# A gated cross-attention block: the scaled rows go through a DMA into a float32r tile and are transposed as float32r

## What is computed

```python
q = einsum('bsd,od->bso', layernorm(x), W) + b
attn_logits = einsum('bqd,bkd->bqk', q, ctx) + (1 - mask) * -1e9
x = x + tanh(g_xattn) * einsum('bqk,bkd->bqd', softmax(attn_logits), ctx)
x = x + tanh(g_ffn) * einsum('bsi,oi->bso', layernorm(x), sign(weight))
```

## Time and profile before

| | |
|---|---|
| three timed runs | 298.51, 302.39, 302.82 us; median 302.39 |
| profiled execution | span 297.0 us; its own time is not listed apart from the three; the median is 5.4 us above the span |
| instructions | 9618 |
| busy shares of the span | PE 96%, PEld 93%, DVE 89%, ACT 87%, POOL 72% |
| granted TensorE clock | mean 0.993 of full speed |
| DMA | 44.40 MB, 149 GB/s over the span |

### The profile page before, as it was taken

The page is one execution under the profiler, slowest core; times in us unless marked ns, Lnnn a source line. Parts: engine busy times, 40 slices in busy tenths (PEclk is TensorE's granted clock), DMA queues, the critical chain, the costliest instruction groups (busy, mean ns, idle before and its releaser), DMA issues.

```text
span 297.0 us, 9618 instructions
## 1 busy us (share of the span) xinstructions
PE 286.3 (96%) x2329; PEld 276.6 (93%) x2329; DVE 265.2 (89%) x1167; ACT 258.8 (87%) x740; POOL 214.6 (72%) x585
## 2 busy tenths in 40 slices
PE   6799999999999999999999999999999999999982
PEld 6789999999999999999999999999999999999972
DVE  4669999999999999999999999999999999999883
ACT  2689999999999999999999999999999999999841
POOL 2546877877787778777777877777787777778543
PEclk9889999999999999999999999999999999999999
DMA  5941464646356544544565453545545444541212
GB/s 130 298 134 42 144 186 152 184 135 186 127 146 184 184 150 146 169 139 146 168 184 154 144 174 125 162 159 184 167 137 174 153 141 146 185 152 70 74 54 89
DMA packets 33539, 44.40 MB, mean 149 GB/s; under 512 B 3504, under 2 KB 17136, under 8 KB 33520
## 3 DMA queue, kind: packets, MB, share of 16 engines
q1 hardware_dynamic: 33520, 44.19, 47.7%
HBM read 27.40 MB, written 16.78 MB: 149 GB/s over the span
## 4 chain that ended last, share of the span: by engine, by line
PE 91%; DMA 2%; SPq 1%; POOL 1%; issue 1%; DVE 1%; ACT 1%; POOLq 0%; ACTq 0%
PE ffn_ps L670 20%; PE pv_ps L652 18%; PE l_ps L636 16%; PE ctx_ps L571 11%; PE xt_ps L604 9%; PE x1t_ps L642 9%; PE pt_ps L617 5%; PE ctx_ps L563 3%; DMA ctx_v<-in_ctx_dram 2%; POOL y L318 0%; POOL rstd L282 0%; DVE x_lo L535 0%; SPq L212 0%; DVE c L524 0%; ACT ffn_scaled L398 0%
## 5 line engine op out<-in xcount | busy, mean ns | idle before, releaser
L282 POOL TENSOR_TENSOR rstd<-ve,minus_half 128x2 f32<-128x2 f32 x128 | 89.1, 696 | 10.0
L636 PE MATMUL l_ps<-m_sb,x_t 128*128 128x77 f32 x512 | 79.0, 258 | 0.3 <-ACT x_t L379 0.3
L344 ACT ACTIVATE xs<-x_in,shift,rstd 128x256 f32<-128x256 f32 x128 | 75.6, 592 | 0.0
L636 PEld LDWEIGHTS l_ps<-m_sb,x_t 128*128 128x128 f32 x512 | 74.8, 191 | 0.6 <-ACT x_t L379 0.6
L642 PE MATMUL x1t_ps<-ident,x 128*128 128x128 f32 x256 | 68.8, 273 | 0.0
L652 PE MATMUL pv_ps<-ctx_v,p_t 77*128 77x256 f32 x256 | 66.1, 380 | 0.0
L670 PE MATMUL ffn_ps<-wf_t,x_hi 128*128 128x256 f32 x256 | 56.2, 301 | 2.5 <-DVE x_lo L535 2.4
L543 DVE SCALAR_TENSOR_TENSOR x<-pv_ps,c,x_in 128x256 f32<-128x256 f32 x128 | 55.5, 475 | 0.4 <-PE pv_ps L652 0.4
L535 DVE TENSOR_TENSOR x_lo<-x1t_ps,x_hi 128x512 fp32r<-128x512 f32 x64 | 44.2, 691 | 12.3 <-ACT x_hi L405 8.8
L318 POOL TENSOR_TENSOR y<-ffn_scaled,x 128x256 f32<-128x256 f32 x64 | 46.6, 728 | 8.2 <-ACT ffn_scaled L398 8.2
L431 DVE BATCH_NORM_STATS2 st<-x_in 128x6 f32<-128x256 f32 x128 | 47.5, 413 | 4.7 <-DMA x_in<-in_x_dram 4.6
(11 more groups left out here) (49 smaller groups left out, 478.9 us busy)
## 6 DMA issues: line engine op xcount, KB each, us to landing
x_in<-in_x_dram SPq DMA_DIRECT2D x64, 256.0 KB, 2.7
out_dram<-y SPq DMA_DIRECT2D x64, 256.0 KB, 2.0
ctx_v<-in_ctx_dram SPq DMA_DIRECT2D x32, 154.0 KB
mask_in<-in_mask_BxSxS_ik_dram SPq DMA_DIRECT2D x32, 154.0 KB, 3.1
wq_raw<-in_L_xattn_W_dram SPq DMA_DIRECT2D x1, 256.0 KB, 2.9
wf_raw<-in_L_ffn_weight_dram SPq DMA_DIRECT2D x1, 256.0 KB, 6.2
bq_col<-in_L_xattn_b_dram SPq DMA_DIRECT2D x1, 1.0 KB, 2.7
g_raw<-in_g_xattn_dram SPq DMA_DIRECT2D x1, 0.5 KB, 3.7
```

What stands on the lines that cost most here:

```text
L282: pool.tensor_tensor(res[:, i], ve[:, i], minus_half[:], ALU.pow).then_inc(res_done, 1)
L344: act.activation(xs[:, n % 2, j], x_in[:, n % N, j], ACT.Identity, scale=rstd1[:, n % R, j:j + 1], bias=shift1[:, n % R, j:j + 1]).then_in ...
L636: ins = pe.matmul(l_ps[:, j * K:(j + 1) * K], x_t[:, r % 2, c, j * P:(j + 1) * P], m_sb[:, c, r % R], start=(c == 0), stop=(c == C - 1))
```

## The change

A second tile `xs_r` of type float32r stands beside `xs`, and a second identity `ident_r` of type float32r. ScalarE still writes `xs`. SyncE then copies the 256 KB of a batch from `xs` to `xs_r` with one DMA, and TensorE waits for that DMA's semaphore and transposes `xs_r` with `ident_r`, with the PSUM tile read as float32r. In slot r the copy of batch r+1 comes first in SyncE's program, ahead of the slot's loads and store; it waits for both activations of `scale_rows` of that batch. VectorE copies the identity once, before its first statistics.

```diff
+        ident_r = sb("ident_r", [P, P], F32R)
+        xs_r = sb("xs_r", [P, 2, T, D], F32R)
+        xs_moved = [sem(f"xs_moved{i}") for i in range(2)]
...
             load_x(0, 4)
 
+            def move_xs(t0, n):
+
+                i = n % 2
+                sp.wait_ge(xs_done, T * (t0 + n + 1))
+                sp.dma_start(xs_r[:, i].bitcast(F32), xs[:, i]).then_inc(xs_moved[i], DMA)
+
+            move_xs(0, 0)
+
             def slot(t0, r):
                 t = t0 + r
+                if exists(t0, r + 1):
+                    move_xs(t0, r + 1)
                 if exists(t0, r + AHEAD):
...
+            dve.wait_ge(ident_ready, 2)
+            dve.tensor_copy(ident_r[:], ident[:]).then_inc(ident_r_ready, 1)
             stats1(0)
...
             def transpose_x(t0, n):
 
-                pe.wait_ge(xs_done, T * (t0 + n + 1))
+                pe.wait_ge(xs_moved[n % 2], landed(t0, n, 2))
                 at_least(pe, xt_done, t0 + n)
                 for c in range(C):
                     for j in range(T):
-                        ins = pe.transpose(xt_ps[:, c, j * P:(j + 1) * P],
-                                           xs[:, n % 2, j, c * P:(c + 1) * P], ident[:])
+                        ins = pe.transpose(xt_ps[:, c, j * P:(j + 1) * P].bitcast(F32R),
+                                           xs_r[:, n % 2, j, c * P:(c + 1) * P], ident_r[:])
                 ins.then_inc(xt_psum, 1)
 
+            pe.wait_ge(ident_r_ready, 1)
             transpose_x(0, 0)
```

More of the change, by code:

```diff
@@ L125, in flamingo_block @@
         half_ready = sem("half_ready")
+        ident_r_ready = sem("ident_r_ready")
         gate_ready = sem("gate_ready")
```

## The result

The changed kernel is slower: 309.29 us median (307.61 to 310.61), the kernel before beside it 301.05 us, a ratio of 1.029 with a 95% interval from 1.021 to 1.037. The forecast was 300.0 us, slightly faster than before; the time is inside the range of 295 to 318, but on the other side. The profiled execution took 310.22 us with a span of 308.2, 11.2 us more than before. That is more than the 8.2 us between the medians. Executions of one kernel differ: nineteen of the kernel before, beside e1 to e4, took 297.7 to 304.5 us, with a mean granted clock of 0.996 in the shortest and 0.972 in the longest. The profile before (clock 0.993) is one of the short ones, the profile after has a mean clock of 0.968.

A forecast was written before the change was run, and what follows sets the result against it. TensorE, busy for 96% of the span, was taken to set the pace. The span of 297.0 less 7.1 (steady slots) plus 4.7 (start) gave 294.6, and 5.4 from span to median made 300.0 us; 80% range 295 to 318.

The forecast's parts named there:

- Part 1: TensorE's four transposes of scaled rows: float32r cuts their spacing from 0.109 to 0.075 us, saving 0.14 us per slot.
- Part 3: Next late engine: TensorE waits about 0.05 us for x1's low part in one slot per pair; 31 pairs save 7.1 us.
- Part 2: Steady slots: SyncE's reaction, a 2.0 us DMA and TensorE's reaction total 2.2 us, fitting the 2.30 us before the transposes.
- the first one: Rival: the copy's DMA lands late, at 2.7 us pairs take 9.20 and the time is 325; chance 0.30 for above 308.4.
- Part 4: Start: the first copy queues behind fourteen start-up DMAs, first transposes at about 13.6 us; costs 4.7 us, between 3 and 6.5.
- 5.4 us from span to median: Amount by which the median before lay above the profiled span, added to the predicted span of 294.6 to give 300.0 us.
- the third rival: TensorE's float32r transposes are slower than plain ones, 0.22 us a piece, adding 26 us, 333 with the start; chance 0.04.

The follow-up runs named there:

- e1: Changed kernel without the copy: ScalarE writes the float32r tile itself, float32r transposes stay; 298.12 us, ratio 0.992 to the kernel before.
- e4: As e3, with ScalarE scaling the rows half a slot sooner and the copy issued ahead of the store; 298.84 us, ratio 0.999 to the kernel before.
- e7: Changed kernel with 50 unread identity transposes filling TensorE's gap ahead of the first batch's transposes; 305.78 us, ratio 1.017 to the kernel before.
- e6: As e4, with the first 24 slots written out instead of the first 8; 298.61 us, ratio 0.992 to the kernel before.
- e5: As e3, with the first 24 slots written out instead of the first 8; 304.48 us, ratio 1.013 to the kernel before.
- e3: Changed kernel, but the first two batches are transposed from xs in float32 without a copy; 303.47 us, ratio 1.012 to the kernel before.
- e8: As e1, with 18 unread identity transposes in TensorE's gap ahead of slot 0; 293.94 us, ratio 0.979 to the kernel before.
- e2: Changed kernel with the copy alone: xs_r is float32 and transposed with the float32 identity; 312.92 us, ratio 1.044 to the kernel before.

## Why the prediction was wrong

**Part 1, the transposes: right in kind, mis-sized.** Where TensorE has waited, the four loads lie in 0.40 us and one lasts 0.142, so they start 0.086 apart instead of the 0.075 taken, within the bounds of 0.067 and 0.12. In an undisturbed slot the first of the three distances stays what it was, 0.130, and the distances behind it fall from 0.108 to 0.086, three of them up to the first feed-forward load. That is 0.07 us a slot where the text had four times 0.034, or 0.14. Part 3's next late engine, the low part of x1, did not show in the steady stretch: the gain there is 0.07 x 62 = 4.3 us instead of 7.1, and the difference is the size of this term. The Trainium skill puts a weight load at its columns / 1.2 ns ("TensorE: Matmul & The Clock Gate", "LDWEIGHTS (loading the stationary operand)"), an estimate of 107 ns for 128 columns; these start 86 ns apart, so the trace does not agree.

**Part 2, the wait for the copy: the failed step.** The sum of 2.2 us came out at 2.36 (SyncE 0.03 instead of 0.15, the DMA 2.29 instead of 2.0, TensorE 0.04), and even so it cost nothing in an undisturbed slot. That was partly luck: the end of the scaling came 1.70 us behind the transposes' first load, as the text had it, and only because the slot stayed at 4.08 us instead of 4.01 was there room for 2.36. What failed is that the step took one landing time for all 64 copies, the median. With so small a margin the tail decides, and the tail stood in the trace of before: the view of the tile x_in gives 2.5/2.7/8.2 us from issue to landing, that of y 2.0/2.0/4.1. The 8.2 is a load of the crowded start; after 20 us a load took up to 4.7 and a store 4.1, both beside a fetch. A late load cost nothing there, since it had more than a slot to spare; a late copy is paid in full, because it sits in the loop from transposes to transposes. The single long slots cost about 5 us in batches 5 to 18 and 2 to 3 at the end. A part of the latter is the last slot, which takes 3.47 us without the copy and 4.04 with an undisturbed one (e7). None of the rivals had this: the first one had all copies slow, not a few. The time of 309.29 lies where that rival had its chance of 0.30, above 308.4, but by another way: the pairs are 8.48 us, not above 8.6. e4 and e6 showed that room for the copy removes it, e5 that more fetches increase it.

**Part 4, the start: right in kind, half the size.** The first transposes came at 14.6 us (13.6 was taken), the second batch's at 20.2 (18.7). Up to there the copy queued behind the start-up loads as described. The text then let the start cost 4.7 us in all, and it cost 8.4 by batch 4. What it left out is a start at the lower clock: slots 2 and 3 took 5.9 and 5.1 us, where they had 4.4 and 4.1. The gap of 7 us is not needed for it, since e1 and e3 have the low clock without that gap and take 4.0 and 4.5 us more than before up to batch 4. Taking the copy out of the start gives back 3.9 (e3), filling the gap 1.4 (e7), by the profiles. Why TensorE's start is idler in e1, e3 and e4 than in the kernel before is open; in e8, where it is filled, nothing of the 4 us is left.

**The sum.** -4.3 instead of -7.1, +8.4 instead of +4.7, and some +7 where nothing stood make the 11.2 us between the profiles. Some 3 of these are not in the medians, 301.05 and 309.29. The text had met the same thing in its 5.4 us from span to median: in the executions listed, before and after, time and span differ by 1.7 to 2.6 us, so the rest of it was a profiled execution shorter than the median one. In the third rival 0.11 x 4 x 62 is 27 and not 26, which changes nothing. What the prediction got right, besides the gain of the transposes: that the copies' traffic and the loads issued later cost nothing in the steady stretch, and that the first scaled rows are not held up by the identity's copy (their copy is issued at 8.0 us, where ScalarE ended at 8.2 before).

## What to carry to other kernels

A DMA put between two engines inside the loop that sets the pace must be sized by its slowest landing, not by its median; read the maximum of issue-to-landing for DMAs of the same size behind the start, and see whether the late ones fall on instruction fetches. Writing out 16 more slots raised these from seven to twelve here. Give it room by issuing its producer half a slot sooner: that cost no instruction here and made the copy nearly free. Look at the first 30 us by themselves, and compare starts at the same granted clock, before a loss there is put down to the change. And if the producer can write the type itself, the copy isn't needed at all.

## What the runs showed of the hardware

- Float32r transposes of 128 columns start 0.086 us apart, float32 ones 0.109, while a float32r matmul of 256 columns starts every 0.12 and the float32 product of the same size needs 0.43. A transpose thus gains far less from float32r than a product does.
- A DMA of 256 KB from SBUF to SBUF lands after 2.29 us in the median, some 0.2 more than the store to DRAM and 0.4 less than the load.
- A fetch of 16 KB of instructions took 0.88 to 1.85 us over all runs. Copies of 256 KB issued close to one landed after up to 4.05 us instead of 2.29 in the changed kernel; in the copies issued at 41.5, 73.8 and 270.9 us fifteen of the sixteen parts had arrived by 2.31 us and the last alone was late.
- TensorE's clock stayed at 2.4 GHz from 8 to 28 us in e8, where the gap ahead of slot 0 is filled with transposes, and was at 1.2 GHz for 13.7 us in the profiled execution of e1, where it isn't.
- The record of the granted clock can lack its start: in e2 the windows read 1.00 from 14 to 28 us, while the four weight loads of a batch's transposes take 0.72 us (at 15.19) and 0.84 (at 21.05) instead of the 0.49 of the steady stretch.
